# The seam between images and the second attention stage reordered in an attention and FFT-convolution kernel

## What is computed

```python
x = x + L0(_gn(x))      # _gn: group norm, 32 groups, over channels and pixels of an image
x = x + L1(_gn(x))

# L0, linear attention, 6 heads of 64:
q, k = rope(conv1x1(x, Wq, bq)), rope(conv1x1(x, Wk, bk)); v = conv1x1(x, Wv, bv)
q = elu(q * scale) + 1; k = elu(k) + 1
kv = einsum('bhnd,bhne->bhde', k, v); k_sum = k.sum(axis=2)
out = einsum('bhnd,bhde->bhne', q, kv) / (einsum('bhnd,bhd->bhn', q, k_sum) + 1e-06)
return conv1x1(out, Wfc, bfc)

# L1:
t = conv1x1(x, w_in); t = irfft2(rfft2(8x8 patches of t) * fft_filter)
t = depthwise 3x3 convolution of t, 'SAME'
g = gelu(t[:, :192]) * t[:, 192:]
return conv1x1(g, w_out)
```

## Time and profile before

| | before |
|---|---|
| median of the runs | 3801.42 us |
| the profiled execution's own time | 3797.91 us |
| its span | 3795.8 us |
| mean granted TensorE clock | 0.984 |
| TensorE matmul busy | 3484.6 us (92%) |
| DVE busy | 3188.5 us (84%) |
| ACT busy | 1627.6 us (43%) |
| POOL busy | 1954.3 us (51%) |
| L791, one product of the rope, mean | 0.55 us |
| L963, the wide gate, mean | 0.69 us |
| L623, rounding to `g_hi`, mean | 0.63 us |

### The profile page before, as it was taken

How to read it: one execution, slowest core, us unless ns; L and a number is a source line. 1 busy time by engine, 2 the same in 40 slices (tenths; PEclk the granted TensorE clock), 3 DMA queues, 4 the chain that set the end, 5 groups by cost and what they waited for, 6 DMA issues and landing times. The chain is left out here.

```text
span 3795.8 us, 50800 instructions
## 1 busy us (share of the span) xinstructions
PE 3484.6 (92%) x18272; PEld 3038.6 (80%) x18272; DVE 3188.5 (84%) x4863; ACT 1627.6 (43%) x2781; POOL 1954.3 (51%) x1242
## 2 busy tenths in 40 slices
PE   4998999989998899988999899998999989899899
PEld 4987779877797778977789777996769967699676
DVE  7986989879898798987979878898789977888777
ACT  1432744337342473324633256332554326533164
POOL 2543655536455464554645546455465445554454
PEclk9999999999999999999999999999999999999999
DMA  5214322143311332123321233213332133221322
GB/s 209 67 40 152 109 100 67 51 150 110 100 66 59 133 125 92 59 75 127 123 85 66 85 124 117 92 51 100 117 109 92 51 116 117 100 86 56 131 99 104
DMA packets 186282, 371.51 MB, mean 98 GB/s; under 512 B 7946, under 2 KB 9010, under 8 KB 185778
## 3 DMA queue, kind: packets, MB, share of 16 engines
q1 hardware_dynamic: 186034, 368.26, 28.6%
HBM read 267.56 MB, written 100.66 MB: 97 GB/s over the span
## 5 line engine op out<-in xcount | busy, mean ns | idle before, releaser
L438 POOL TENSOR_TENSOR t<-t 128x768 f32<-128x768 f32 x256 | 533.1, 2083 | 531.8 <-DVE t L791 531.8
L1072 PE MATMUL bank<-w_hi,x_hi 128*128 128x384 f32 x2322 | 785.1, 338 | 4.0 <-ACT x_hi L542 4.0
L1073 PE MATMUL bank<-w_lo,x_hi 128*128 128x384 f32 x2322 | 786.1, 339 | 0.0
L431 POOL TENSOR_TENSOR x_lo<-xa,x_hi 128x512 fp32r<-128x512 f32 x363 | 498.3, 1389 | 552.5 <-ACT x_hi L542 552.5
L948 DVE SCALAR_TENSOR_TENSOR bank<-big,wdw,bank 128x512 f32<-128x512 f32 x1072 | 752.6, 745 | 20.2 <-PE bank L1240 17.3
L547 ACT ACTIVATE t<-t 128x768 f32<-128x768 f32 x256 | 217.4, 849 | 888.8 <-POOL t L438 888.8
L499 POOL TENSOR_TENSOR prod<-prod 128x512 f32<-128x512 f32 x320 | 411.7, 1287 | 317.6 <-ACT prod L634 298.9
L801 DVE SCALAR_TENSOR_TENSOR kt<-t 128x384 f32<-128x384 f32 x256 | 546.1, 2133 | 0.0
L1077 PE MATMUL bank<-w_hi,x_lo 128*128 128x384 f32 x2322 | 537.2, 339 | 0.5 <-POOL x_lo L431 0.5
L1072 PEld LDWEIGHTS bank<-w_hi,x_hi 128*128 128x128 f32 x2322 | 438.2, 189 | 5.2 <-ACT x_hi L542 4.4
L1073 PEld LDWEIGHTS bank<-w_lo,x_hi 128*128 128x128 f32 x2322 | 437.3, 188 | 0.0
(11 more groups left out here) (129 smaller groups left out, 7106.7 us busy)
## 6 DMA issues: line engine op xcount, KB each, us to landing
xr<-x SPq DMA_DIRECT2D x128, 768.0 KB, 4.7
xa<-x SPq DMA_DIRECT2D x66, 768.0 KB, 6.3
x_scratch<-xr SPq DMA_DIRECT2D x64, 768.0 KB, 3.5
xa<-x_scratch SPq DMA_DIRECT2D x64, 768.0 KB, 6.1
xr<-x_scratch SPq DMA_DIRECT2D x64, 768.0 KB, 4.9
out<-xr SPq DMA_DIRECT2D x64, 768.0 KB, 3.5
big<-x SPq DMA_DIRECT2D x8, 768.0 KB, 10.3
w_raw<-wqkv_t SPq DMA_DIRECT2D x1, 1728.0 KB, 7.2
```

Source lines behind the costliest of these rows:

```text
L431: nc.gpsimd.tensor_tensor(dst, src, hi, ALU.subtract).then_inc(s_lo, 1)
L438: nc.gpsimd.tensor_tensor(a, a, b[:, :, ::-1, :], ALU.add).then_inc(s_add, 1)
L1072: nc.tensor.matmul(dst, hi(k), whi(k), start=first and k == 0, stop=False)
L1073: nc.tensor.matmul(dst, hi(k), wlo(k), start=False, stop=False)
```

## The change

In stage B, DVE no longer adds the residual of channel block 2, but for the last chunk: ACT writes the product with its bias from PSUM into a new SBUF buffer `proj` (in memory that stage B didn't use), between its second and third copy to `qt_hi`, and POOL adds `proj` to `xr` behind `times_ksum`. Two semaphores, `s_proj` and `s_sum`, carry this; SyncE's store waits for `s_sum` too. DVE's `divide_q` is split: `denominators` ends with the reciprocal, `divide_q` is the multiplication behind it. DVE's step is now `denominators` and `divide_q` of chunk c + 1, `low_q` block 2 of chunk c, two residuals of c - 1 and their statistics, `low_q` blocks 0 and 1 of c + 1, the third statistics. TensorE's step is the high products of output blocks 0 and 1, their low products, transposes of groups 0 and 1 of chunk c + 1, output block 2, transposes of group 2.

At the seam TensorE's step 8 is `project` of T0, taps of block 0, the three output blocks of chunk 6, taps of block 1. Output block 1 of chunk 6 goes to a second bank (`INVB`). In step 9 two of the three blocks of `project` of T1 stand ahead of the output blocks of chunk 7, the third behind them; the thirty warming matmuls are gone. The wait for the residuals stands behind `project` of T2. DVE does the three residuals of chunk 6 in step 9, one behind each pair of the first six taps of chunk 7, and `rope` of T0 ahead of the last three taps. Behind the last image no engine works for a next one. `tapdiag` is laid out in another way with the same twelve matrices.

```diff
-        (w_raw, ), (qn, ), (t1, t2, kt), (tb, gb, prod, gel) = overlay(
+        (w_raw, ), (qn, proj), (t1, t2, kt), (tb, gb, prod, gel) = overlay(
...
+            [("qn", [P, 2, TPC, C], fp32), ("proj", [P, CHUNK], fp32)],
...
-        def out_bank(m, last=False):
-
-            return (ACCB[2], ACCB[0])[m % 2] if last else OUTB
+        def out_bank(c, m):
+
+            if c == NCH - 1:
+                return (ACCB[2], ACCB[0])[m % 2]
+            return INVB if c == NCH - 2 and m == 1 else OUTB
...
@@ SyncE, part_b
                         wait(s_res, (i * 16 + c) * 3 + 3)
+                        if c - 2 < NCH - 1:
+                            wait(s_sum, i * (NCH - 1) + c - 1)
                         sp.dma_start(chunk_of(x1_v, i, c - 2), xr[:, par]).then_inc(s_st[par], 16)
...
@@ GpSimd, part_b
                         times_ksum(c + 1, 1 - par)
+                    if c > 0:
+                        gp.wait_ge(s_xr[1 - par], (i * 12 + 5 + (c - 1) // 2) * 16)
+                        gp.wait_ge(s_proj, i * (NCH - 1) + c)
+                        nc.gpsimd.tensor_tensor(xr[:, 1 - par, 2], xr[:, 1 - par, 2], proj[:, :], ALU.add).then_inc(s_sum, 1)
...
@@ ScalarE, part_b
                     for j in range(KB):
+                        if j == KB - 1 and c > 0:
+                            act.wait_ge(s_out, (i * 16 + c) * 3 + 6)
+                            act.wait_ge(s_sum, i * (NCH - 1) + (c - 1))
+                            nc.scalar.activation(proj[:, :], bank[4 + 3 * (1 - par)][:, :], ACT.Identity,
+                                                 bias=bfc_c[:, 2:3]).then_inc(s_proj, 1)
                         act.wait_ge(s_tp, n * 3 + (j + 7))
                         nc.scalar.activation(qt_hi[:, par, j], bank[(par + j) % 2][:, :], ACT.Copy).then_inc(s_qt, 1)
...
@@ VectorE, the division split in two
-                def divide_q(c, par):
+                def denominators(c, par):
...
+                def divide_q(c, par):
+
+                    n = i * 8 + c
+                    by_head = qn[:, par].rearrange("p t (h d) -> p (t h) d", d=HD)
                     dve.wait_ge(s_nd, n * 3 + 3)
...
@@ VectorE, residual
-                        ins.then_inc(s_res, 1)
+                        ins.then_inc(s_res, KB - m if m == blocks[-1] and len(blocks) > 1 else 1)
...
@@ VectorE, stage B
+                denominators(0, 0)
                 divide_q(0, 0)
...
-                low_q(0, 0)
+                low_q(0, 0, (0, 1))
 
                 def part_b(c, h, edge, par):
-                    if within(edge, 0, NCH, 1):
+                    r, more = (i * 16 + c) * 3, c + 1 < NCH
+                    if more:
+                        denominators(c + 1, 1 - par)
                         divide_q(c + 1, 1 - par)
-                    if edge == NCH:
-
+                    if c < NCH:
+                        low_q(c, par, (2,))
+                    if 1 <= c < NCH:
+                        residual(i * 16 + c - 1, i * 12 + 4 + h + par, 1 - par, True, blocks=(0, 1))
+                        for k in range(2):
+                            dve.wait_ge(s_res, r + (4, 6)[k])
+                            nc.vector.bn_stats(bn_x1[:, k, c - 1, :], xr[:, 1 - par, k])
+                    if more:
+                        low_q(c + 1, 1 - par, (0, 1))
+                    if 1 <= c < NCH:
+                        dve.wait_ge(s_sum, i * (NCH - 1) + c)
+                        nc.vector.bn_stats(bn_x1[:, 2, c - 1, :], xr[:, 1 - par, 2]).then_inc(s_x1s, 1)
+                    if c == NCH:
                         for m in range(KB):
                             residual(i * 16 + c - 1, i * 12 + 4 + h + par, 1 - par, True, blocks=(m,))
-                            dve.wait_ge(s_res, (i * 16 + c) * 3 + (m + 4))
+                            dve.wait_ge(s_res, r + (m + 4))
                             ins = nc.vector.bn_stats(bn_x1[:, m, c - 1, :], xr[:, 1 - par, m])
                         ins.then_inc(s_x1s, 1)
-                        return
-                    if within(edge, 0, NCH, -1):
-                        residual(i * 16 + c - 1, i * 12 + 4 + h + par, 1 - par, True)
-                    if within(edge, 0, NCH, 1):
-                        low_q(c + 1, 1 - par, (0, 1))
-                    if within(edge, 0, NCH, -1):
-                        dve.wait_ge(s_res, (i * 16 + c) * 3 + 6)
-                        for k in range(KB):
-                            ins = nc.vector.bn_stats(bn_x1[:, k, ds(c - 1, 1), :].rearrange("p c s -> p (c s)"),
-                                                     xr[:, 1 - par, k])
-                        ins.then_inc(s_x1s, 1)
-                    if within(edge, 0, NCH, 1):
-                        low_q(c + 1, 1 - par, (2,))
...
@@ VectorE, part_c: step 9 of an image (last), and the products of chunk 6 left out of step 8
+                    if last:
+                        for m, early in enumerate((LAST[0:2], LAST[2:4], LAST[4:6])):
+                            for q, k in early:
+                                tap(c - 2, q, k, last)
+                            add_out(3, m)
+                        gate_narrow(c - 2, last)
+                        if i + 1 < images:
+                            rope((i + 1) * NT, 0, 0)
+                        for q, k in LAST[6:]:
+                            tap(c - 2, q, k, last)
+                        gate_wide(c - 2, last)
+                        for m in range(KB):
+                            add_out(2, m)
+                        return
...
-                    if gated:
-                        add_out(2, 0, last)
+                    if 2 <= c < NCH:
+                        add_out(2, 0)
...
@@ TensorE, project and the wait moved
-            def project(T, m, par, j):
+            def project(T, m, par, j, blocks=range(3)):
...
-                for b in range(3):
+                for b in blocks:
...
-                pe.wait_ge(s_res, i * 48 + 6)
-
                 def part_a(c, h, edge, par):
                     T = (i * 8 + c) * 4
                     first = edge == 0
                     m = i * 16 + c
                     project(T + 2, m, par, 2)
+                    if first:
+                        pe.wait_ge(s_res, i * 48 + 6)
                     add_kv(T, 0, first=first)
...
@@ TensorE, stage B
+                def out_high(c, par, m):
+
+                    r, n = (i * 16 + c) * 3, i * 8 + c
+                    if m < 2 or c < 2:
+                        pe.wait_ge(s_res, r + ((1, 3, 3)[m] if c >= 2 else m + 1))
+                    else:
+                        pe.wait_ge(s_proj, i * (NCH - 1) + (c - 1))
+                    for j in range(KB):
+                        if m == 0:
+                            pe.wait_ge(s_qt, n * 3 + (j + 1))
+                        for w in (mout_hi, mout_lo):
+                            nc.tensor.matmul(bank[2 + 3 * par + m][:, :], w[:, j, m * P:(m + 1) * P], qt_hi[:, par, j],
+                                             start=(j == 0 and w is mout_hi), stop=False)
+
+                def out_low(c, par, m):
+
+                    for j in range(KB):
+                        if m == 0:
+                            pe.wait_ge(s_ql, (i * 8 + c) * 3 + (j + 3))
+                        ins = nc.tensor.matmul(bank[2 + 3 * par + m][:, :], mout_hi[:, j, m * P:(m + 1) * P], qt_lo[:, par, j],
+                                               start=False, stop=(j == KB - 1))
+                    ins.then_inc(s_out, 1)
+
                 def part_b(c, h, edge, par):
-                    r = (i * 16 + c) * 3
-                    for m in range(KB):
-                        if m == KB - 1 and within(edge, 0, NCH, 1):
-                            transpose_q(c + 1, 1 - par)
-                        pe.wait_ge(s_res, r + (m + 1))
-                        dst = bank[2 + 3 * par + m][:, :]
-                        cols = slice(m * P, (m + 1) * P)
-                        for j in range(KB):
-                            if m == 0:
-                                pe.wait_ge(s_qt, (i * 8 + c) * 3 + (j + 1))
-                            nc.tensor.matmul(dst, mout_hi[:, j, cols], qt_hi[:, par, j], start=(j == 0), stop=False)
-                            nc.tensor.matmul(dst, mout_lo[:, j, cols], qt_hi[:, par, j], start=False, stop=False)
-                        for j in range(KB):
-                            if m == 0:
-                                pe.wait_ge(s_ql, (i * 8 + c) * 3 + (j + 3))
-                            ins = nc.tensor.matmul(dst, mout_hi[:, j, cols], qt_lo[:, par, j], start=False, stop=(j == KB - 1))
-                        ins.then_inc(s_out, 1)
+                    more = c + 1 < NCH
+                    out_high(c, par, 0)
+                    out_high(c, par, 1)
+                    out_low(c, par, 0)
+                    out_low(c, par, 1)
+                    if more:
+                        transpose_q(c + 1, 1 - par, (0, 1))
+                    out_high(c, par, 2)
```

(65 more changed lines are left out.)

79 lines of the change are left out of this document (37 added, 42 removed).

## The result

The changed kernel takes 3680.41 us (median of four runs, 3677.71 to 3683.6) against 3801.27 (3799.98 to 3806.09) of the kernel before on the same chip: ratio 0.968, 95% interval 0.9663 to 0.9697. The forecast was 3669, range 3640 to 3712. The profiled execution took 3683.6 us, the longest of the four; its span fell from 3795.8 to 3681.8, by 114 us where the sum said 135 (the medians fell by 121).

The account below looks back on a forecast made before the run. DVE's own queue was taken to bound stage B, 8.84 of 9.65 us per chunk. Savings of 70 + 59 + 6 = 135 from 3797.9 gave 3663, 3667 with the 3.5 us timing offset, 3669 with 2 for ties; range 3640 to 3712.

Parts of the forecast that it names:

- Order of B, and the idle 0.81 us: Stage B, one chunk: new order removes DVE's 0.81 us wait and one 0.69 us residual; step 9.65 to 8.16 us.
- The tie: Stage B: POOL's product lets the reduce start at s + 6.15, DVE arrives at s + 6.17; s is the reciprocal's start.
- POOL's add at no cost: Stage B: POOL's 1.3 us add, from about s + 6.5 (s: reciprocal's start), hidden by DVE's reduce; cost 0.
- rival 1: Stage B: POOL's add stands in the loop, reduce or `qn` waits, 1.3 us in five steps; 3716 us, chance 0.08.
- ACT's Identity at 0.6: Stage B: ACT's new write from PSUM to `proj` takes 0.6 us, bounds 0.5 and 1.1.
- End of B: After the last reciprocal: store, load and last residual of chunk 7 keep their distances; nothing gained or lost.
- Seam: Between images: project T2 starts 8.8 us earlier, 8.4 taken per seam; seven seams give 59 us.
- DVE's lag: Start of A: DVE enters 3.5 us closer to TensorE, makes it up while TensorE waits 0.4 at the first `add_kv`.
- Tail: End of the last image: no projections for an image that doesn't exist; 6 us saved, range 2 to 10.
- Group norm "keeps its length": Behind stage B: statistics and group norm keep their lengths, so no change there.
- Rival 3: Stage B and seam: short waits put TensorE at its lower clock, 1.2 GHz; about 4090 us, chance 0.03.
- Sum: Whole launch: 70 (B) + 59 (seam) + 6 (tail) = 135 us off 3797.9.

Follow-up runs that it names:

- e1: Changed kernel with the sum by head written to its own tile, row stride 9, and read there by the epsilon add (L873); 3649.44 us, ratio 0.9598.
- e4: Changed kernel with the rope of the next image's T1 on DVE ahead of the last three residuals; 3675.91 us, ratio 0.9668.
- e12: e1 with 22 instead of 14 warming matmuls between stage B and the first group average; 3635.3 us, ratio 0.9567.
- e2: Changed kernel with 18 instead of 14 warming matmuls behind stage B; 3680.22 us, ratio 0.968.
- e5: Changed kernel with the edits of e1, e2 and e4 together; 3649.77 us, ratio 0.9598.
- e8: Changed kernel with only an unused tile ahead of the large SBUF buffers, which moves these by 108 bytes; 3662.55 us, ratio 0.9638.
- e9: Changed kernel with e1's edit, but the small tile allocated behind all large buffers, which stay unmoved; 3656.47 us, ratio 0.9619.
- e7: Kernel before the change with 12 instead of 14 warming matmuls behind stage B; 3810.41 us, ratio 1.0039.

## Why the prediction was right, step by step

- **Order of B, and the idle 0.81 us**: held. The step without the wait is 8.13 (e1), where the prediction had 8.13 for the loop through POOL and 8.16 for DVE's queue. The tie was real: in e1 DVE has no idle time in a step, and its reduce starts at 1628.74, 0.04 us behind the end of POOL's product. TensorE's pauses of 0.37 us ahead of `low_q`'s matmuls leave no idle time on DVE.
- **POOL's add at no cost**: this is the step of B that failed. It was placed at s + 6.5 to 7.9 and costed at 0 "with 0.7 us left" ahead of the next `qn`. It ran from s + 6.97 to 8.26. The margin was reckoned against POOL's next instruction only, not against what DVE does at s + 7.92: L873 waits for POOL's end. Price 0.20 us per step, 8.33 instead of 8.13, and 0.8 in the second step of five images: 12.7 us over the launch. This is rival 1 at another instruction and, in most steps, at less than a sixth of its price: not the 1.75 us reduce, which never waited (1.740 to 1.754 us in all 64), but the 0.18 us add behind it, and only for the rest of POOL's add. The Trainium skill, "SBUF — State Buffer", section "Who interferes with whom", has both halves: `tensor_reduce` never takes the shared pair on trn2, `tensor_scalar` can, when its operands suit. The trace agrees: beside POOL's add the reduce keeps its length, and the `tensor_scalar` of L873 ends with POOL's add in all 48 cases. The prediction quoted the one and did not apply the other to L873.
- **ACT's Identity at 0.6**: measured 0.69, hidden.
- **End of B**: held; the load of chunk 7 sets it, and the whole stretch is 0.55 us shorter per image, not 0.
- **Seam**: held. Predicted 25.4 us from the taps to project T2, measured 25.5; DVE's wait 4.1, measured 4.07. The wait of 0.4 us at the first `add_kv` came one step later as 0.71 for ACT's `vt`, and A grew by 1.0 us per image: net 53.4 us of 59 (8.6 less 1.0 per seam against 8.4). The prediction made this loss DVE's lag, at 0.4; e4 took the wait away and got 0.1 of the 1.0 back. By the trace DVE's lag now hangs on the load of x (e4), which the prediction let move with the last store; no run tested it.
- **Tail**: 6 predicted, 7.8 measured. About half lies where the prediction had nothing: stage C of the last image is 3.6 us shorter, since DVE no longer normalises in it for an image that doesn't exist. The end behind it gives the other 4.1.
- **Group norm "keeps its length"**: wrong by 17.3 us, the largest miss. Rival 3 had looked for the clock in B and at the seam. At the seam it stayed up (1.00 from the taps to project T2), and in B it was down only in the first two steps, where it had been down before too; it fell in a stretch whose own code was not touched. e12 gives all of it back.
- **Sum**: of 135 us 21 are missing: 17.3 in group norm, 5.6 at seam and A, 5.0 in the steps of B (L873, and a second step of 9.2 us in five images, 8.1 in e1), less 6.7 that came back at the end of B, in the tail and ahead of the first B. The time stayed inside the range, 11 us above the forecast. That the group norm's 17 us did not carry it out is owed to the width of the range, which had no term for it. Three of the prediction's sums are a little off and change nothing: the good ends add up to 144 us (not 146), the bad ends give 3714 (not 3712), and rival 1's five steps cost 6.5 us (not 6.2).

## What to carry to other kernels

When work moves to POOL, list every DVE instruction that runs beside it, the smallest too: here a 0.18 us add that met a 1.3 us POOL operation waited out the rest of it, and its operand in a tile of its own and another layout took the wait away. When TensorE's clock was low upstream of it, the same wait grew from 0.2 to 0.8 us. After any change ahead of a stretch in which TensorE barely works, read the granted clock of that stretch again; here filling the wait ahead of it wholly paid, and half filling it was worth nothing in the medians (e2, e5). Where a launch repeats TensorE work thousands of times, try a shift of the tiles by itself before crediting an edit that also moved them.

## What the hardware showed beyond that

An unused tile of 108 bytes ahead of the large tiles made the same 2304 matmuls 335 ns instead of 338 on average, stage A 1.6 us shorter per image and the launch 18 us shorter (e8); e9, with the tile last and A as before, shows that A's gain comes of the shift and not of the tile. Which tile's place matters, and why, is not shown. Two warming matmuls fewer per image in the kernel before made it 0.39% slower (e7, interval 0.23 to 0.56), though they are 0.5 us less work; its eight runs had a mean granted clock of 0.976 to 0.984, those of the kernel before 0.982 to 0.987.
